# Relative-position scores through DRAM: one run per partition for both steps of a pair, in place of two rows each

## What is computed

```
AC    = einsum('bhld,bhmd->bhlm', q + u_bias, k)
BD    = einsum('bhld,hrd->bhlr',  q + v_bias, r)          # r: 2L-1 relative positions
score = (AC + _rel_shift(BD)) / sqrt(DEPTH)               # row l takes BD[l, L-1-l : 2L-1-l]
attn  = softmax(score); out = einsum('bhlm,bhmd->bhld', attn, v); return out @ Wo + bo
```

## Time and profile before

| | us |
|---|---|
| median of three runs | 1694.87 |
| lowest and highest run | 1694.71, 1704.96 |
| the profiled execution's own time | 1699.04 |
| its span, first to last instruction | 1697.2 |
| relative heads with spills in flight | about 1156 to 1618 |
| gated feed-forward behind them | about 1618 to 1697 |

### The profile page before, as it was taken

One profiled execution on the slowest core, in us unless ns is written; L12 is line 12 of the kernel. 1 busy time (PEld: TensorE's weight loads), 2 busy tenths in 40 slices (PEclk: granted clock), 3 DMA queues, 4 the chain that ended last, 5 costly groups with the idle time before them and its releaser, 6 DMA issues. The chain is left out here.

```text
span 1697.2 us, 36694 instructions
## 1 busy us (share of the span) xinstructions
PE 1473.9 (87%) x12580; PEld 938.1 (55%) x12580; DVE 1234.0 (73%) x3703; ACT 1119.9 (66%) x2657; POOL 440.1 (26%) x442
## 2 busy tenths in 40 slices
PE   4688998989989885588888888769999999999996
PEld 2255555556555553366666666646555555555564
DVE  4367777777777765688888788663877878878755
ACT  1267676776767761567777677627888787887742
POOL 0333333333333313454544444330000000000001
PEclk9599999999999997899999999877999999999998
DMA  1677777788777745111001110007999999999920
GB/s 41 163 185 194 188 186 197 185 194 190 186 186 189 194 108 187 22 30 31 19 20 31 25 27 19 12 13 219 324 315 315 309 314 300 313 314 302 292 73 25
DMA packets 154904, 272.97 MB, mean 161 GB/s; under 512 B 27920, under 2 KB 31200, under 8 KB 154592
## 3 DMA queue, kind: packets, MB, share of 16 engines
q1 hardware_dynamic: 154720, 270.63, 56.3%
HBM read 148.03 MB, written 112.98 MB: 154 GB/s over the span
## 5 line engine op out<-in xcount | busy, mean ns | idle before, releaser
L519 ACT ACTIVATE a_Pm<-a_Pm,a_nm 128x272 f32<-128x272 f32 (+3 forms) x512 | 266.7, 570 | 167.3 <-DVE a_nm L441 166.7
L441 DVE CUSTOM_DVE_ANT_0 a_Pm<-ps,a_mask 128x272 f32<-128x272 f32 (+3 forms) x512 | 237.7, 503 | 92.3 <-PE ps L358 90.8
L1768 ACT COPY r_BD<-ps 128x320 f32<-128x320 f32 x512 | 200.4, 428 | 92.1 <-PE ps L1621 46.7
L1895 DVE CUSTOM_DVE_ANT_0 r_Sx<-ps,r_Sx 128x512 f32<-128x512 f32 x256 | 176.8, 691 | 108.8 <-PE ps L1634 107.2
L1621 PE MATMUL ps<-r_R,r_qv 32*128 32x320 f32 x1024 | 234.2, 498 | 3.2 <-ACT r_BD L1768 2.3
L358 PE MATMUL ps<-a_Kst,a_Qst 128*128 128x272 f32 (+4 forms) x640 | 200.6, 409 | 15.4 <-DMA a_Kst<-bounce 15.1
L1634 PE MATMUL ps<-r_K,r_qu 32*128 32x256 f32 x1024 | 199.7, 436 | 3.4 <-DVE r_nb L1895 3.4
L358 PEld LDWEIGHTS ps<-a_Kst,a_Qst 128*128 128x128 f32 x640 | 113.4, 193 | 146.3 <-issue 62.6
L1775 ACT ACTIVATE r_Sx<-r_Sx,r_nb 128x512 f32<-128x512 f32 x256 | 187.6, 733 | 7.9 <-DVE r_nb L1895 7.9
L1904 DVE COPY r_PT<-ps 128x512 f32<-128x512 f32 x256 | 175.9, 687 | 4.6 <-PE ps L1644 4.0
L373 PE MATMUL ps<-m_ident,a_Pm 128*128 128x128 f32 x1280 | 170.5, 278 | 1.6 <-ACT a_Pm L519 0.7
(11 more groups left out here) (204 smaller groups left out, 2745.9 us busy)
## 6 DMA issues: line engine op xcount, KB each, us to landing
spill<-r_BD SPq DMA_DIRECT2D x256, 288.0 KB, 5.0
r_Sx<-spill SPq DMA_DIRECT2D x128, 512.0 KB, 5.7
a_Kst<-bounce SPq DMA_DIRECT2D x128, 264.0 KB, 4.9
a_Qst<-bounce SPq DMA_DIRECT2D x128, 256.0 KB, 4.6
bounce<-a_kh SPq DMA_DIRECT2D x32, 264.0 KB, 3.5
bounce<-a_kl SPq DMA_DIRECT2D x32, 264.0 KB, 4.1
bounce<-a_qh SPq DMA_DIRECT2D x32, 256.0 KB, 5.7
bounce<-a_ql SPq DMA_DIRECT2D x32, 256.0 KB, 6.0
```

Of the source, the lines that this page charges most:

```text
L441: nc.vector.tensor_tensor_reduce(out=Pm[:, u % 2, qt, 0:w], in0=S[:, S_of[qt]:S_of[qt] + w], in1=mask[:, N + AV - w:N + AV], scale=-SCALE, ...
L519: nc.scalar.activation(row, row, ACT.Exp, scale=-1.0, bias=nm[:, u % 2, qt:qt + 1]).then_inc(exp_done, 1)
L1768: nc.scalar.copy(BD[:, m % BUFS, j, HW * half:HW * half + HW], ps[:, BDB[k % 3], 0:HW]).then_inc(bd_ev, 1)
L1895: nc.vector.tensor_tensor_reduce(out=row, in0=ps[:, AC + n % 2, :], in1=row, scale=-SCALE, scalar=-BIG, op0=ALU.add, op1=ALU.min, accum_ou ...
```

## The change

Both steps of a pair lie behind one another in DRAM in each partition's row of 1,280 elements. The spill is one DMA of all 128 partitions, one run of 1,280 elements (5,120 bytes) for each, 640 KB. The read back has a pitch of 1,279 elements and one run of BW + N = 1,152 elements (4,608 bytes) for each partition, 576 KB; the first 512 elements are those of the first step, the last 512 those of the second, and 128 between them are not used. `Sx` grows by 128 elements in each of its six buffers. `yb` becomes a view of `xT[:, B - 1]` and `Norm` writes its output in place, so two tiles of 2 KB for each partition fall away. The semaphore counts go from 32 to 16 for each pair.

```diff
-    spill = [nc.dram_tensor(f"spill{k}", (2, P, BW), F32, kind="Internal").ap() for k in range(SCRATCH)]
+    spill = [nc.dram_tensor(f"spill{k}", (P, 2 * BW), F32, kind="Internal").ap() for k in range(SCRATCH)]
...
-    Sx = s.sb("Sx", [P, SCRATCH, 2, N])
+    Sx = s.sb("Sx", [P, SCRATCH, BW + N])
...
-    yb = s.sb("yb", [P, NT, D])
-    nrm = Norm(s, "n")
+    yb = xT[:, B - 1].rearrange("p (t n) -> p t n", t=NT)
+    nrm = Norm(s, "n", out=yb)
...
-                    rows_of = spill[k % SCRATCH].rearrange("t p n -> p t n")
-                    sp.dma_start(rows_of[0:HP2, :, HP2:BW], BD[0:HP2, k % BUFS, :, HP2:BW]).then_inc(wr[k % BUFS], 16)
-                    sp.dma_start(rows_of[HP2:P, :, 0:BW - HP2], BD[HP2:P, k % BUFS, :, 0:BW - HP2]).then_inc(wr[k % BUFS], 16)
+                    sp.dma_start(spill[k % SCRATCH], BD[:, k % BUFS].rearrange("p t n -> p (t n)")).then_inc(wr[k % BUFS], 16)
                 if k >= 1:
                     m = k - 1
-                    sp.wait_ge(wr[m % BUFS], 32 * (m // BUFS + 1))
+                    sp.wait_ge(wr[m % BUFS], 16 * (m // BUFS + 1))
...
-                    skew = bass.AP(tensor=a.tensor, offset=P - 1, ap=[[BW - 1, P], [P * BW, 2], [1, N]])
+                    skew = bass.AP(tensor=a.tensor, offset=P - 1, ap=[[2 * BW - 1, P], [1, BW + N]])
...
-                row = Sx[:, n // 2 % SCRATCH, n % 2, :]
+                row = Sx[:, n // 2 % SCRATCH, BW * (n % 2):BW * (n % 2) + N]
...
-                    nrm.apply(nc, link, nrm.out, yb)
+                    nrm.apply(nc, link, yb, yb)
                     xs = X[:, b * NT:b * NT + NT, :]
-                    nc.vector.tensor_tensor(xs, xs, nrm.out[:], ALU.add).then_inc(x_done, 1)
+                    nc.vector.tensor_tensor(xs, xs, yb, ALU.add).then_inc(x_done, 1)
```

More of the change, by code:

```diff
@@ L583, with __init__ @@
 class Norm:
-    def __init__(self, s, name):
+    def __init__(self, s, name, out=None):
         self.st = s.sb(name + "_st", [P, NT, 6])
@@ L589, in __init__ @@
         self.rstd = s.sb(name + "_rstd", [P, NT])
-        self.out = s.sb(name + "_out", [P, NT, D])
+        self.out = s.sb(name + "_out", [P, NT, D]) if out is None else out
     def variance(self, nc, link, x, eps):
@@ L1520, in relative_heads @@
     BDB, AC, TB, O = (0, 1, 7), 2, 4, 6
-    HW, HP2 = BW // 2, P // 2
+    HW = BW // 2
     EB, XB, QB, KB = 0, (2, 3, 0, 1), (4, 5, 4, 5), (6, 7, 6, 7)
@@ L1643, in turn @@
                 for j in range(NT):
-                    ins = nc.tensor.transpose(ps[:, TB + n % 2, P * j:P * j + P], Sx[:, n // 2 % SCRATCH, n % 2, P * j:P * j + P],
+                    ins = nc.tensor.transpose(ps[:, TB + n % 2, P * j:P * j + P], Sx[:, n // 2 % SCRATCH, BW * (n % 2) + P * j:BW * (n % 2) + P * j + P],
                                               c["ident"][:])
@@ L1765, in relative @@
                 if m >= BUFS and j == 0 and half == 0:
-                    act.wait_ge(wr[m % BUFS], 32 * (m // BUFS))
+                    act.wait_ge(wr[m % BUFS], 16 * (m // BUFS))
                 act.wait_ge(bd_ready, k + 1)
@@ L1807, in gate @@
                     for k in range(BUFS):
-                        act.wait_ge(wr[k], 32 * len(range(k, PAIRS, BUFS)))
+                        act.wait_ge(wr[k], 16 * len(range(k, PAIRS, BUFS)))
                 act.wait_ge(up_ready, n + 1)
@@ L1893, in add @@
                     v.wait_ge(exp_done, n - 7)
-                row = Sx[:, m % SCRATCH, n % 2, :]
+                row = Sx[:, m % SCRATCH, BW * (n % 2):BW * (n % 2) + N]
                 nc.vector.tensor_tensor_reduce(out=row, in0=ps[:, AC + n % 2, :], in1=row, scale=-SCALE, scalar=-BIG, op0=ALU.add,
```

## The result

| | us |
|---|---|
| median before, in the same job | 1698.08 |
| median of the changed kernel, four runs | 1723.22 |
| ratio, 95% interval | 1.0145 [1.0103, 1.0186] |
| the profiled execution's own time, its span | 1727.14, 1725.3 |

The change makes the kernel 25 us slower. I had forecast 7.5 us slower.

What follows compares the result with a forecast made beforehand. DMA turnaround on SP was taken to set the pace in about two pairs of three, TensorE close behind. Extra bytes added 7.5 us, other terms nothing: 1694.87 + 7.5 = 1702 us, range 1684 to 1722.

Steps and rivals of the forecast that it cites:

- What bounds the kernel: On SP, DMA turnaround (landing to next landing but one) sets the pace in about two pairs of three; TensorE close behind.
- rival A: SP's loop: fewer issues and all ports shorten the turnaround more than bytes lengthen it; 12 us faster, 1683 us; chance 0.22.
- Bytes and rate: Spill and read: 11.8% more bytes a pair, at 405 GB/s for longer runs against 382 before; +0.15 us a pair.
- The count of pairs: SP's loop: the added time counts in 100 pairs, between 76 and all 119.
- How it enters: SP's loop: one read and one spill in two pairs, the rest latency; +0.075 us each pair, +7.5 us.
- The issue: SP: one spill issue less saves 0.60 us a pair, but the read covers it; costed at nothing.
- The port rule: Spill DMAs: half spills of 64 partitions reach only half the ports, so one whole spill would gain; given nothing.
- B: DMA engines, not turnaround, are the bound; all added transfer time falls on each pair: 1713 to 1735 us, chance 0.23.
- C: The waits have enough slack and TensorE's order sets the time, so nothing moves: 1695 us, chance 0.10.
- Moved steps: Waits moved on SP, `Norm` in place and `yb` in `xT` add no cost; taken as 0.
- The forecast of the waits: ScalarE's wait for spills should grow from 42.7 to over 50 us.
- The forecast rate: DMA rate over the stage should rise to 335 to 345 GB/s, share still 0.95.

Runs made afterwards that it cites:

- e6: The changed kernel with SP's read moved one pair later, two pairs behind: 1684.06 us, ratio 0.9937 to the kernel before.
- e5: The kernel before with SP's read moved one pair later, two pairs behind: 1693.25 us, ratio 0.9990.
- e7: The kernel before with four buffers of BD in place of three, SP's order as before: 1688.89 us, ratio 0.9963.
- e8: The kernel before with four buffers of BD and the read two pairs behind: 1691.48 us, ratio 0.9982.
- e3: The changed kernel's bytes in the DRAM layout before, two short runs per partition in spill and read: 1720.45 us, ratio 1.0148 to before.
- e1: The changed kernel's single spill, but the read as before in two rows of 2,048 bytes: 1695.81 us, ratio 1.0011 to before.
- e2: The changed kernel's read, with the spills as before in two DMAs, in the new layout: 1706.92 us, ratio 1.0081 to before.
- e4: The changed kernel with its spill issued as two DMAs of 64 partitions each: 1719.78 us, ratio 1.0151 to before.
- e10: e3 with SP's read two pairs behind: 1679.83 us, ratio 0.9898 to the kernel before.
- e11: e1 with SP's read two pairs behind: 1680.18 us, ratio 0.9901 to the kernel before.

## Why the prediction was wrong

**What bounds the kernel: right, but overstated.** The turnaround on SP was named as the pace-setter, and e6 shows it for the changed kernel. For the kernel before it was overstated: removing the hold or its effect gained at most 9 us (e5, e7, e8), where rival A gave 12. (The slices with a DMA share of 0.9 are 29 to 38, not 28 to 38.)

**Bytes and rate: right in size, for a reason that does not hold.** It is 1,216 KB a pair, and two stretches gave 401 and 411 GB/s for a full share against the 405 that I took. Over 1200 to 1600 us, in half-microsecond slices with a share above 0.98, the mean for a full share is 345 GB/s before and 367 after. Both are below my 382 and 405, but 1.245 MB / 367 less 1.114 MB / 345 is +0.16 us a pair, as in the sum. My reason was the longer runs; e3, without a run over 2,560 bytes, has 369. That the term came out is partly luck.

**The count of pairs: right.** I took 100; SP's rows give 96 of 118.

**How it enters: this step failed.** It counted "one read and one spill in two pairs", put +0.15 us on two pairs, +0.075 on each, and took "the rest of the 7.07 us" as latency that stays as it is. Measured were 3.86 against 3.61 us a pair, +0.25, so two pairs grew by 0.5 us, not 0.15; the medians from a read to the next but one, 7.24 and 7.77, say the same. Part of the error is in the count: between the reads of 1401.97 and 1409.98 SP issues two reads and two spills, so the engines move the bytes of both pairs in that time. With both counted the term would be +0.30. The other 0.2 us are in the rest, which was not a constant. SP goes on when the last of the 16 updates of a spill's semaphore has come. In the changed kernel the first came 5.0 and the last 7.2 us behind the issue (medians of 43 spills), 2.4 us apart; in e6 they came 3.1 and 4.7 us behind it, 1.6 apart. Whether the extra 0.2 us lie in this spread or in the start of a read (0.57, then 0.92 busy at 173 GB/s) stays open: the runs change the loop as a whole. Whether the bytes of spill and read add up is also open: e1 and e2 together are 1.0092, the whole is 1.0145, and the intervals leave room for both.

**The issue, at nothing: right in the loop.** e4 equals the changed kernel, one DMA or two.

**The port rule.** I gave it nothing, from the steady rows. Under the hold that stood (e4). With the hold gone, e6, e10 and e11 against e5 fit it, and they fit as well that one spill DMA lets the read behind it be issued and land sooner; no run parts the two. The Trainium skill's page "SBUF — State Buffer", section "Door 1: The DMA port swizzle", has it that partitions 0 to 63 reach 8 of the 16 ports and 64 to 127 the other 8, so that a half spill reaches half of them; the trace before agrees only at the stage's first spill, 194 GB/s.

**The rivals.** B's number was nearest, 1722 against 1723.22 us, by luck, since its reason was wrong: the DMA engines could move more, 352 and 355 GB/s in e6 and e10 where the changed kernel moved 324. A row of mine said so, the 0.68 share at 135 GB/s. The Trainium skill's "HBM Reference", section "Specifications (TRN2)", gives about 358 GB/s as a core's share; no mean over 400 us here went above it, and the short stretches at 393 and 432 GB/s did, so it set no limit on these. A fell: its first condition (a shorter turnaround) did not come. C fell.

**Moved steps.** `Norm` in place and `yb` in `xT` are in e7 and e10 as well, which are faster than before; they cost nothing that shows. No run changes them alone.

The forecast of the waits was right in direction (over 50 us, measured 82.7), and the range ended 1 us below the median. The forecast rate of 335 to 345 GB/s over the stage was missed, 322: it went with a pair that hardly gets longer.

## What to carry to other kernels

When a queue issues one transfer behind the landing of another, price a longer transfer by trying the order, not by its bytes over the bandwidth: here 12% more bytes in another form cost 25 us with the hold, and without it the kernel is 12 us faster than before. Before changing the shape of a transfer, look whether its issue waits for its data or for another transfer's landing; if the latter, put the waiting issue behind the one that is ready. When a time spans several rounds of a loop, count every transfer issued in it, and do not take what is left over as a constant. And when an experiment puts a wait back, look whether it slows the kernel by the same waits as the original, and not only by as much.

## What the runs showed of the hardware

The busy share of the DMA engines did not tell how much room there was: over 1200 to 1600 us it was 0.96 at 310 GB/s, 0.95 at 324, 0.96 at 352 and 0.99 at 355, in the same stage of four kernels. A high share can go with few bytes, 0.92 at 173 GB/s behind a read's issue; that the engines there wait for the read's first data fits the place, and is not shown. The 16 updates that tell of one spill's landing were 2.4 us apart in the changed kernel, in the median. A wait that disappears need not give time back: e5 took ScalarE's wait from 40.8 to 2.7 us, late reads came in its place, and the kernel stayed within 0.4%.
